# Routing written first, with context frequencies, projections and weight turning moved into its waits and behind the experts

## What is computed

```python
x = x + tanh(g_xattn[0]) * L0_xattn(layernorm(x), ctx)   # cross attention, 16 heads of 8, rotary positions
x = x + tanh(g_ffn[0])   * L0_ffn(layernorm(x))          # 8 experts, 2 per sequence
x = x + tanh(g_xattn[1]) * L1_xattn(layernorm(x), ctx)   # autocorrelation attention
x = x + tanh(g_ffn[1])   * L1_ffn(layernorm(x))          # MLP with a gate, 352 wide, blocks rounded to FP4
```

```python
pooled = x.mean(axis=1); logits = pooled @ Wr
top_scores, top_idx = jax.lax.top_k(logits, 2)
weights = jax.nn.softmax(top_scores, axis=-1)
h = gelu(einsum('btd,bkdf->bktf', x, W1[top_idx]) + b1[top_idx])
out = einsum('bk,bktd->btd', weights, einsum('bktf,bkfd->bktd', h, W2[top_idx]) + b2[top_idx])
```

## Time and profile before

| | |
|---|---|
| runs | 314.01, 311.06, 312.22 us; median 312.22 |
| profiled execution | 312.27 us, around a span of 310.5 us |
| TensorE matmuls | 260.1 us busy, 84% of the span, 2126 instructions |
| TensorE weight loads | 199.1 us busy, 64% |
| VectorE | 205.5 us busy, 66%, 556 instructions |
| ScalarE | 163.6 us busy, 53%, 381 instructions |
| GpSimd | 114.7 us busy, 37%, 163 instructions |
| mean granted TensorE clock | 0.943 of full |

### The profile page before, as it was taken

How to read it: one execution, slowest core, us unless ns; L and a number is a source line. 1 busy time by engine, 2 the same in 40 slices (tenths; PEclk the granted TensorE clock), 3 DMA queues, 4 the chain that set the end, 5 groups by cost and what they waited for, 6 DMA issues and landing times.

```text
span 310.5 us, 6172 instructions
## 1 busy us (share of the span) xinstructions
PE 260.1 (84%) x2126; PEld 199.1 (64%) x2126; DVE 205.5 (66%) x556; ACT 163.6 (53%) x381; POOL 114.7 (37%) x163
## 2 busy tenths in 40 slices
PE   2999889999898988999999994987892857598675
PEld 1565257666667935999999993666661424467474
DVE  3499988888986355342322337663989499999951
ACT  1169365666584578775566553762327352434321
POOL 3174549993202103229952202300554303231230
PEclk9999999999999999999999999699997588979957
DMA  7994000000000208676777710000000000001011
GB/s 246 357 387 196 0 3 2 2 2 0 3 2 2 74 2 364 262 303 276 292 291 305 291 70 3 1 0 2 0 0 1 0 2 0 0 17 34 19 34 35
DMA packets 11871, 30.13 MB, mean 97 GB/s; under 512 B 961, under 2 KB 5057, under 8 KB 11713
## 3 DMA queue, kind: packets, MB, share of 16 engines
q1 hardware_dynamic: 11840, 29.75, 25.2%
HBM read 9.75 MB, written 1.05 MB: 35 GB/s over the span
## 4 chain that ended last, share of the span: by engine, by line
PE 53%; DVE 30%; ACT 7%; issue 5%; DMA 3%; POOL 1%; SPq 0%; DVEq 0%
PE ps L1223 10%; PE ps L1214 9%; PE ps L1104 5%; DVE s_region L276 4%; PE ps L1078 4%; PE ps L1091 4%; DVE s_small L225 3%; DVE s_region L680 3%; PE ps L1401 2%; DVE s_small L967 2%; DVE s_region L272 2%; PE ps L1114 2%; PE ps L1283 2%; DMA s_region<-s_wall 2%; PE ps L1379 2%
## 5 line engine op out<-in xcount | busy, mean ns | idle before, releaser
L542 ACT ACTIVATE s_region<-ps,s_region 128x128 f32<-128x128 f32 x144 | 40.8, 371 | 20.5 <-PE ps L1214 20.4
L834 DVE SCALAR_TENSOR_TENSOR s_ctxT<-ps,s_region,s_ctxT 128x64 f32 x72 | 18.1, 281 | 45.7 <-PE ps L1223 45.4
L1214 PE MATMUL ps<-s_region 128*128 128x128 f32 x288 | 37.9, 276 | 0.8 <-DVE s_ctxT L810 0.5
L1223 PE MATMUL ps<-s_region 128*128 128x128 f32 x288 | 38.0, 276 | 0.5 <-ACT s_region L542 0.5
L1214 PEld LDWEIGHTS ps<-s_region 128*128 128x128 f32 x288 | 34.9, 192 | 1.8 <-DVE s_ctxT L810 1.3
L1223 PEld LDWEIGHTS ps<-s_region 128*128 128x128 f32 x288 | 35.0, 192 | 0.9 <-ACT s_region L542 0.7
L1379 PE MATMUL ps<-s_region 128*128 128x352 f32 x64 | 25.9, 558 | 11.3 <-DVE s_region L957 6.1
L283 POOL TENSOR_TENSOR s_region<-s_region,s_small 128x704 f32<-128x704 f32 (+2 forms) x13 | 17.5, 1343 | 47.6 <-DVE s_region L276 47.6
L248 POOL TENSOR_TENSOR s_small<-s_small,s_par 128x4 f32<-128x4 f32 (+3 forms) x14 | 15.5, 1108 | 47.1 <-DVE s_small L231 47.1
L380 POOL COPY s_region<-s_xt 128x64 f32 x72 | 14.9, 240 | 40.2 <-PE ps L1214 21.9
L490 ACT COPY s_region<-ps 128x512 f32<-128x512 f32 x32 | 17.2, 589 | 18.2 <-PE ps L1091 18.2
(11 more groups left out here) (205 smaller groups left out, 507.0 us busy)
## 6 DMA issues: line engine op xcount, KB each, us to landing
s_region<-s_wall SPq DMA_DIRECT2D x36, 514.0 KB, 3.2
s_wall<-wall SPq DMA_DIRECT2D x8, 514.0 KB, 9.2
s_par<-par SPq DMA_DIRECT2D x1, 1316.0 KB, 11.1
s_ctxT<-ctxT SPq DMA_DIRECT2D x2, 512.0 KB, 6.0
s_x<-x SPq DMA_DIRECT2D x2, 512.0 KB, 7.4
out<-s_x SPq DMA_DIRECT2D x8, 128.0 KB, 1.8
s_region<-ffn SPq DMA_DIRECT2D x1, 560.0 KB, 3.6
s_par<-par SPq DMA_DIRECT2D x1, 460.0 KB, 3.8
```

Source lines behind the costliest of these rows:

```text
L542: ins = act.activation(hg[j % 3][:, c, :], ps[:, j % 3, RPT * S * c:RPT * S * (c + 1)], ACT.Gelu, bias=wbuf[j % 6][:, FF + FC * D + c:FF + ...
L834: dve.scalar_tensor_tensor(row, ps[:, 4 + j % 2, S * k:S * k + S], w, row, ALU.mult, ALU.add).then_inc(m["acc_done"], 1)
L1214: ins = mm(ps[:, j % 3, RPT * S * c:RPT * S * (c + 1)], w[:, P * c:P * c + P], xg[j % 4], start=True, stop=True)
L1223: ins = mm(ps[:, 4 + j % 2, 0:RPT * S], w[:, FF + D * c:FF + D * c + D], hg[j % 3][:, c, :], start=(c == 0), stop=(c == FC - 1))
```

## The change

The routing is rewritten so that its own steps stand first on every engine, and other work is put between them in small pieces.

- VectorE normalises tiles 8 to 11 before the last write of x, ScalarE tiles 12 to 14. `turn_tokens(0)` and `(1)` move into the last steps of the first attention. The sums of sequences 0 to 15 are taken by VectorE from the turned tokens (`pool_group`), those of tiles 8 to 15 by products as before. The context's frequencies are written tile by tile (`context_tiles`) between the routing's products, in the banks of `CTX_BANK`.
- The counts per expert no longer stand behind the softmax weights; the weights and what comes from them (`wt`, `ohw`, `wtT`, `wB`) are made after the packed codes. ScalarE, not VectorE, fills the accumulator with b2; GpSimd sets its spare rows to zero at the start.
- `context_kv(0)` and `(1)` stand before the experts, `(2)` to `(7)` in the second attention. Each has its bias added in PSUM by a product of the identity with 8 columns (`frequency_bias`), and is copied once; `kfs` and `vfs` are gone, and VectorE reads `kf` and `vf` with the real and imaginary part in reverse order instead.
- The queries have their bias added in PSUM too, and `products` reads them there; `qf` is not written. `queries` and `sum_heads` are interleaved differently. The turning of the MLP's weights moves from the experts' end behind the last projection. The bias of the output is added to x (`bias_added`) between the products instead of between the rolled values.
- GpSimd normalises tiles 12 to 15 after the experts, ScalarE 0 to 11, and `to_frequency` waits for each tile instead of four.
- In the MLP `gate_up(q)` multiplies both gates of a pair, then both up halves, with a semaphore of its own for the gates, for which silu waits; `x_round(1)` and `(2)`, `(3)` and their turns stand one pair later or earlier than before. The block maxima `hmx` are written at every second word. `preload(Silu)` stands before the second lags copy, `preload(Exp)` right after the experts.

```diff
+CTX_BANK = (4, 6, 7, 4)
-        kf, kfs, vf, vfs = (carve(2048 * i, B, 2, DFT) for i in range(4))
+        kf, vf = carve(0, B, 2, DFT), carve(4096, B, 2, DFT)
-        hmx, hsc, hin = ([sm(2 * NH) for _ in range(3)] for _ in range(3))
+        hsc, hin = ([sm(2 * NH) for _ in range(3)] for _ in range(2))
+        hmx = [sm(2 * NH, 2)[:, :, 0] for _ in range(3)]
...
+            normalise(pool, 12, 16, m["xn_c_late"], 10)
...
+            def kv_turned(n):
+                act.wait_ge(m["kv_done"], n + 1)
+                z, bank = (kf, 6 + n % 2) if n < G4 else (vf, 2 + n % 2)
+                act.copy(z[:, 8 * (n % G4):8 * (n % G4) + 8].rearrange("p b c s -> p (b c s)"), ps[:, bank, :]).then_inc(m["kv_used"], 1)
...
-            for g in range(2 * G4):
-                act.wait_ge(m["kv_done"], g + 1)
...
+            kv_turned(0)
+            act.wait_ge(m["b2_done"], 1)
+            act.copy(acc[:, 0:B, :], ps[:, 2, 0:B].unsqueeze(2).broadcast_to([P, B, S])).then_inc(m["acc_ready"], 1)
+            kv_turned(1)
...
             exp_lead(0)
             heads_turned(1)
+            kv_turned(4)
             turn_gx(0)
+            kv_turned(5)
             exp_lead(1)
+            preload(ACT.Silu)
             turn_gx(1)
+            kv_turned(6)
+            kv_turned(7)
+            weights_turned(0)
+            weights_turned(1)
             y1_turned(0)
...
-                act.wait_ge(m["gu_done"], 2 * q + 2)
+                act.wait_ge(m["gate_done"], q + 1)
...
-            normalise(dve, 8, 12, m["xn_b_late"], 4)
+                if t == 14:
+                    normalise(dve, 8, 12, m["xn_b_late"], 4)
...
+            def pool_group(g):
+                dve.wait_ge(m["tr2_used"], g + 1)
+                dve.tensor_reduce(pooled[:, 8 * g:8 * g + 8], xt[:, 512 * g:512 * g + 512].rearrange("p (b s) -> p b s", s=S),
+                                  AX, ALU.add).then_inc(m["pooled_ready"], 1)
...
-            dve.tensor_copy(acc[:, 0:B, :], ps[:, 2, 0:B].unsqueeze(2).broadcast_to([P, B, S])).then_inc(m["acc_ready"], 1)
-            dve.memset(acc[:, B:ROWS, :], 0.0).then_inc(m["acc_ready"], 1)
...
-                dve.wait_ge(m["q_used"], g + 1)
-                dc.step(dve.tensor_scalar(qf[:, rows, 0, 0], qf[:, rows, 0, 0], b64[:, 0:1], None, ALU.add))
-                dve.wait_ge(m["kv_biased"], 2)
+                dve.wait_ge(m["q_done"], g + 1)
+                dve.wait_ge(m["kv_used"], g + 1)
+                qps = ps[:, 2 * (g % 2) + 1, :].rearrange("p (b c s) -> p b c s", c=2, s=DFT)
+                for z, k in ((pp, kf[:, rows]), (pq, kf[:, rows, ::-1, :])):
+                    dve.tensor_tensor(z[:, rows], qps, k, ALU.mult).then_inc(m["pp_done"], 1)
...
+            out_and_stats(0)
+            roll_values(4)
             roll_values(5)
-            out_and_stats(0)
+            out_and_stats(1)
+            x_scale(0)
             roll_values(6)
             roll_values(7)
-            out_and_stats(1)
+            x_round(0)
...
+            def frequency_bias(bank, n, rows=slice(0, 8)):
+
+                pe.wait_ge(m["bias64_ready"], 1)
+                out = ps[:, bank, :].rearrange("p (b c s) -> p b c s", c=2, s=DFT)[:, rows, 0, 0]
+                return mm(out, ident, b64[:, n, rows], start=False, stop=True)
...
+            def context_kv(n, first=0, last=4):
...
+                mm(ps[:, bank, P * first:P * last], pc("wk1" if n < G4 else "wv1"), ctxF[:, lo + P * first:lo + P * last], start=True, stop=False)
+                ins = frequency_bias(bank, 1 + n // G4, slice(2 * first, 2 * last))
...
+            context_kv(2)
+            turn_experts(0)
+            turn_experts(1)
+            context_kv(3)
...
+            context_kv(4)
             correlate(1)
...
             turn_lags(0)
             spectrum(0)
+            context_kv(5)
             spectrum(1)
             turn_lags(1)
             spectrum(2)
+            context_kv(6)
             spectrum(3)
+            context_kv(7)
+            turn_weights(0)
+            turn_weights(1)
             out_product(0)
+            turn_weights(2)
```

441 lines of the change are left out of this document (226 added, 215 removed).

## The result

The changed kernel takes 0.989 of the time before (95% interval 0.985 to 0.994), with medians of 311.25 us against 313.66 us over twelve runs each. The ratio is smaller than these two medians say, since it leaves out executions in which the clock was granted less than usual. The same program, measured twice more beside the experiments, gave 0.988 (0.983 to 0.992) and 0.988 (0.982 to 0.994); the medians alone differ by 2.4, 3.8 and 2.9 us in the three. On the 312.22 us that the forecast starts from, the ratios give 308.3 to 308.9 us; the forecast was 308.2, with a range of 304.8 to 311.8.

A forecast was written before the change was run, and what follows sets the result against it. TensorE bounds the experts, VectorE the MLP, and a chain of hand-overs the second attention between. The terms -6.5 + 2.0 + 0.4 = -4.1 us take 312.27 to 308.2 us, with a range of 304.8 to 311.8.

The forecast's parts named there:

- The routing: Before the experts: logits 4.6 us earlier, the expert list 7.2 earlier at 107.1, the slot codes 8.2 earlier at 109.6.
- rival C: Behind the experts: TensorE's clock falls again, five pieces at 0.5 us more each, giving 310.7 us; chance 0.2.
- Experts to the read of the second correlation: Second attention's beginning: the second correlation is read at 215.0 instead of 216.75 us, on the clock of before.
- Read to first attention_out: Second attention: projections, copies and weights on the chain put VectorE's first attention_out at 232.5, 5.1 us later than 227.44.
- the exponent waits: ScalarE, second attention: the second half's exponent stands behind the sixth projection's copy, so first values are multiplied 1.4 us later.
- The 0.2: Before the first gated product: 0.2 us allowed for TensorE at half clock in the thin stretch.
- The 1.0 taken off for L972: VectorE, MLP: maxima read with a stride shorten waits beside GpSimd; 1.0 us taken, between 0 and 2.1.
- rival B: MLP: L972 keeps all 2.1 us of its waits despite the stride, giving 309.2 us; chance 0.25.
- Rival A: MLP and clock: the stride frees L972 and the half clock stays away, giving 306.9 us; chance 0.15.
- step 2: Start of the experts: first second-layer product at 117.4, held by ScalarE's chain to Gelu; 6.5 us gained, bounds 5.8 and 7.3.
- Rival D: Second attention: moved projections and copies lie in series on the chain, up to 11.4 us, giving 317.6 us; chance 0.08.
- Rival E: Start of the experts: weights, not Gelu, hold the experts, a stall of a microsecond, giving 309.2 us; chance 0.07.

The follow-up runs named there:

- a_fill: The changed kernel with three unread products of 256 columns added on TensorE in the wait behind the first part of the first projection; 0.996 of before (0.991 to 1.001).
- a_again: The changed kernel with nothing edited, measured again as partner of the other runs; 0.988 of before (0.983 to 0.992).
- a_control: The changed kernel with nothing edited, measured a second time as partner; 0.988 of before (0.982 to 0.994), median 310.1 us.
- a_early: The changed kernel with all eight projections ahead of the experts again, the new routing kept; 1.007 of before (1.004 to 1.011).
- a_late: The changed kernel with the last two projections and the MLP weights' turning behind the first output product on TensorE and ScalarE; median 309.5 us, no ratio.
- a_fill2: The changed kernel with 31 unread products of 128 columns in TensorE's waits between out_product(1) and the first gates; 0.990 of before (0.986 to 0.994).

## Why the prediction was right, point by point

**The routing.** List 107.1 forecast, 106.84 measured; codes 109.6 and 109.20. Each of its terms holds to 0.4 us: from the logits to the counts 1.4 (L1215 at 104.89) where I had 1.6, from there to the list 1.95 for 1.9, from the list to the codes 2.4 for 2.5.

**Who starts the experts.** The first hidden product was forecast for 113.1 and came at 114.31, the first second-layer one for 117.4 and came at 118.70. The order on the engines was as told; the missing term is the clock, and at half clock it is TensorE and not the Gelu that comes last. In a_fill, where it is full, the two come at 112.04 and 116.30, with the logits at 102.80 instead of the forecast's 103.6: 9.2 and 13.5 us behind the logits, where the forecast had 9.5 and 13.8. There TensorE waits for the Gelu, 0.77 us, as I had it. So the chain was priced to 0.3 us and the halved clock costs 1.7 more (15.2 from logits to first second-layer product). I had looked for a fall of the clock only behind the experts (rival C). In a_again too it fell behind the thinned routing; in a_control, where it had fallen earlier, it did not, and there it is 13.5 us again. The experts ended 5.3 to 6.0 us earlier, not 6.5, and took 62.5 us from the first second-layer product to the last, 62.8 before.

**Experts to the read of the second correlation.** Forecast 1.7 us shorter, measured 2.7 (27.39) at full clock, 1.1 to 1.2 where the clock is halved for 3.4 us (29.03, 28.84). Before had 6.8 us of halved clock there and I compared with that as it stood, so how much of the 2.7 is the order and how much the clock isn't shown; nor does any run take back the queries in PSUM or GpSimd's share of the normalising alone. The sum had two slips: its parts (1.3, 1.16 and 0.2) give 2.7 and not 2.8, and less 1.3 that is 1.4 and not 1.7.

**Read to first attention_out.** Forecast 17.5 us (215.0 to 232.5), measured 17.60, and 15.91 at full clock. The agreement of the first is luck, since the forecast has no half clock in this stretch: it is 1.6 too long. One term that was priced too high is the projection with its bias, at 1.3: in a_early, at full clock, they follow one another every 1.08 us (117.01, 118.09, 119.17, 120.25). VectorE's idle ahead of it is 5.83 us, ended by TensorE, where I said over 5. The cause is shown by a_late: 4.8 us of the stretch are the last two projections and the weights. That the exponent waits was right; that it delays anything was wrong for this kernel, since TensorE was later still.

**First attention_out to first gated product.** Forecast 18.0, with 0.2 in it for a half clock; measured 19.18, 19.99 and 18.41. The 0.2 was too small: at 0.82 and 0.83 of the clock it is 1.2 to 2.0 more, at 0.91 0.4, and a_fill2 with the clock full has 17.77. The clock's term was mis-sized. The working fits otherwise: silu is no longer what VectorE waits for, but at half clock it still waits for TensorE's up halves, as here in a_again, where sixteen gate and up products took 7.10 us:

```profile
243.98 0.89 DVE L965 TENSOR_TENSOR s_region<-s_region,ps 128x704 f32<-128x704 f32 x1 [1.85 <-PE ps L1432]
```

What I called 17.75 us of VectorE's work before holds 16.36 us of it; the rest, 1.4, are gaps, of which a_fill2 has 1.1.

**The MLP.** Forecast 0.4 us longer; measured 1.6, 3.1 and 1.7. The rounding of 1.4 is there (VectorE busy 43.6 against 42.1). The 1.0 taken off for L972 is not: L980 takes what L972 took. That is the mechanism that I had wrong, beside the exponent's delay, and rival B, at 0.25, had it right (309.2). In a_again 1.6 more are waits of VectorE for up halves made at the halved clock, 1.24 us at the longest.

**The sum.** 4.1 us forecast, 3.3 to 3.9 measured by the ratios. Stage by stage, a_again against the forecast: the experts end 0.5 later than forecast, the next stage is 1.0 shorter, the one after it 1.6 shorter, the third 2.0 longer, the MLP 2.7 longer and the end 2.3 shorter. Errors of 5.2 us one way and 4.9 the other make up the agreement to 0.3. Some 6 of these 10 us (the 2.0, 1.6 of the MLP's and the 2.3) go with where the halved clock happens to lie, so part of the agreement is luck; the execution profiled first, with its clock lower, has no gain at all. One bound was off as well: from A with the upper bound of step 2 the range begins at 306.1 (306.9 less 0.8), not 304.8. Rival A did not come, as the stride frees nothing. Rival C came in part: the clock fell behind the experts too, for 3.4 us, in two of three profiles. Rival D, every projection on the chain, is refuted by the time itself, which is below before's and not above it, and by a_early, which loses 5 to 6 us by having them in front. Rival E did not come: a wait for weights is seen only in a_fill, at full clock, and it is 0.30 us.
